# Attention over eight batches: the next batch's preparation placed among the units of the current one

## What is computed

```python
q = _split_heads(x @ Wq, h)
kv = _split_heads(x @ Wkv, h)
q = q * cos + _rotate_half(q) * sin
kv = kv * cos + _rotate_half(kv) * sin
q = q * d ** (-0.5)
kvs_ccs = jnp.concatenate([kvs[:, :-1], kvs[:, 1:]], axis=2)
lsim = jnp.einsum('csmd,csnd->csmn', qs[:, 1:], kvs_ccs)
lsim = jnp.concatenate([lsim[..., :m], jnp.where(causal, mask_value, lsim[..., m:])], axis=-1)
attn1 = jax.nn.softmax(lsim, axis=-1)
out1 = jnp.einsum('csij,csjd->csid', attn1, kvs_ccs)
out1 = _merge_heads(out1, b, h) @ Wo + bo
```

## Time and profile before

| | us |
|---|---|
| median of three runs | 3045.97 |
| the profiled execution, its own time | 3046.24 |
| its span | 3044.4 |
| TensorE busy | 2202.2 (72%) |
| VectorE busy | 2314.3 (76%) |
| ScalarE busy | 1553.2 (51%) |
| GpSimd busy | 845.2 (28%) |

### The profile page before, as it was taken

The page is one execution under the profiler, slowest core; times in us unless marked ns, Lnnn a source line. Parts: engine busy times, 40 slices in busy tenths (PEclk is TensorE's granted clock), DMA queues, the critical chain, the costliest instruction groups (busy, mean ns, idle before and its releaser), DMA issues. The chain is left out here.

```text
span 3044.4 us, 48644 instructions
## 1 busy us (share of the span) xinstructions
PE 2202.2 (72%) x12865; PEld 1704.6 (56%) x12865; DVE 2314.3 (76%) x5828; ACT 1553.2 (51%) x4161; POOL 845.2 (28%) x1482
## 2 busy tenths in 40 slices
PE   6787888786776878777777777877777775434676
PEld 3444454443444777666676766766766664333444
DVE  5555646556774199999999999999999999993566
ACT  3444434434664455555555555555555554443666
POOL 0000000000000144455544444544444554441000
PEclk8888978778888876677877777777767766565788
DMA  4000000000000000000000000000000000000000
GB/s 148 10 6 10 4 9 10 10 6 0 0 0 0 0 1 0 0 0 0 1 0 0 1 0 0 1 0 0 1 0 0 0 0 0 0 0 0 14 21 21
DMA packets 14137, 21.00 MB, mean 7 GB/s; under 512 B 1280, under 2 KB 12032, under 8 KB 13824
## 3 DMA queue, kind: packets, MB, share of 16 engines
q1 hardware_dynamic: 14080, 20.36, 2.2%
HBM read 12.27 MB, written 4.19 MB: 5 GB/s over the span
## 5 line engine op out<-in xcount | busy, mean ns | idle before, releaser
L1298 POOL TENSOR_TENSOR wu<-U,stg 128x256 f32<-128x256 f32 x512 | 317.8, 621 | 854.4 <-DVE U L1232 854.4
L556 PE MATMUL bank<-U,ident 128*128 128x128 f32 x2080 | 471.2, 398 | 115.4 <-ACT go L768 101.9
L556 PEld LDWEIGHTS bank<-U,ident 128*128 128x128 f32 x2080 | 434.2, 248 | 158.0 <-issue 72.9
L619 PE MATMUL bank<-stack,tm 128*128 128x64 f32 x1792 | 353.4, 387 | 217.4 <-ACT tm L705 217.4
L619 PEld LDWEIGHTS bank<-stack,tm 128*128 128x128 f32 x1792 | 341.9, 297 | 237.2 <-issue 237.2
L905 ACT ACTIVATE xs<-U 128x256 f32<-128x256 f32 x512 | 213.4, 417 | 468.9 <-DVE U L1232 467.4
L1182 DVE TENSOR_REDUCE pn<-xs 128x32 f32<-128x512 f32 x512 | 351.3, 686 | 29.3
L1251 POOL TENSOR_TENSOR stg<-R 128x128 f32 (+1 forms) x65 | 29.7, 457 | 1047.8 <-ACT stg L789 1047.8
L1255 POOL TENSOR_TENSOR kv<-stg 128x256 f32<-128x256 f32 x513 | 317.7, 619 | 1.7
L542 PE MATMUL bank<-wcat,yT 128*128 x1024 | 301.4, 454 | 3.0 <-issue 3.0
L677 ACT ACTIVATE prob<-bank,nmax 128x128 f32<-128x128 f32 x512 | 145.6, 366 | 247.6 <-DVE nmax L1026 246.6
(11 more groups left out here) (179 smaller groups left out, 3994.2 us busy)
## 6 DMA issues: line engine op xcount, KB each, us to landing
out_x<-x SPq DMA_DIRECT2D x8, 512.0 KB, 2.9
x<-in_x SPq DMA_DIRECT2D x1, 3584.0 KB, 16.8
Vs<-V SPq DMA_DIRECT2D x8, 272.0 KB, 3.4
lane<-in_lanes SPq DMA_DIRECT2D x8, 256.0 KB, 3.2
wcat<-in_wcat SPq DMA_DIRECT2D x1, 1792.0 KB, 14.0
Vs<-V SPq DMA_DIRECT2D x8, 204.0 KB, 2.7
wraw<-in_w_up SPq DMA_DIRECT2D x1, 1024.0 KB, 18.7
wraw<-in_w_down SPq DMA_DIRECT2D x1, 1024.0 KB, 10.9
```

Of the source, the lines that this page charges most:

```text
L556: last = pe.matmul(rsum.rearrange("p (t i) -> p t i", i=HD), ident[:, :], steps[:, :, :, j], start=(j == 0), stop=(j == HD - 1))
L619: last = pe.matmul(bank[3 + g][:, e * CH:(e + 1) * CH], tm[:, g * (PB // 2) + e, :, :].rearrange("p a c -> p (a c)"), stack[:, :], start=T ...
L1298: pool.tensor_tensor(ij(wu[:, :]), ij(U[:, half if j else 1 - half, (j - 1) % STEPS, :]), col(stg[:, half, j, TW, :]), ALU.mult).then_inc( ...
```

## The change

`KEEP` goes from 4 to 1, so the mask is written twice. `qT`, `kT`, `V` and `Vs` get a second copy, chosen by the batch's parity; the loop runs over pairs of batches. Batch 0 is prepared ahead of the loop. In the loop, the steps that prepare batch b+1 (`nxt`) stand between the steps of batch b's units, one tile in three slots. In the last iteration they prepare a batch that nothing reads. The normalisation of batch b+2 stands at the end of batch b. Banks change hands: projections use bank 3 alone, head transposes bank 0 alone, the values' product bank 2 alone, and o transposes and the output projection share bank 1. ScalarE copies both q and k. The square root of the variance goes to GpSimd as a power of one half. The scan moves from slot 3 to slot 17. On SyncE, the shift for batch b+1 stands behind the load of lane block b.

| slot w of batch b | TensorE | ScalarE | VectorE |
|---|---|---|---|
| 0 | row transposes of b+1 | | |
| 1 | | row copies | |
| 3, 6, 9, 12 | projection of tile 0 to 3 | | |
| 4, 7, 10, 13 | | | rotation |
| 5, 8, 11, 14 | | V and upper halves | |
| 6, 9, 12, 15 | | | lower halves |
| 7, 10, 13, 16 | transposes of q | | |
| 8, 11, 14, 17 | | copy of q | |
| 9, 12, 15, 18 | transposes of k | | |
| 10, 13, 16, 19 | | copy of k | |
| 13 | | absolute values | |
| 16, 17, 18 | | | statistics; scan; normalisation |

Within a slot VectorE now divides first (slots 5, 9, 13, 17), then takes the maximum, copies `probT`, and then does the steps of the table; the residual addition stays last (7, 11, 15, 19).

```diff
-KEEP = 4
+KEEP = 1
...
-        qT = sb("qT", [P, H // 2, L], F16, mid)
-        kT = sb("kT", [P, H // 2, SEG + L], F16, mid)
-        V = sb("V", [P, NT, H, HD + 1], F32, mid)
-        Vs = sb("Vs", [P, NT, H, HD + 1], F32, mid)
+        qT = sb("qT", [P, 2, H // 2, L], F16, mid)
+        kT = sb("kT", [P, 2, H // 2, SEG + L], F16, mid)
+        V = sb("V", [P, 2, NT, H, HD + 1], F32, mid)
+        Vs = sb("Vs", [P, 2, NT, H, HD + 1], F32, mid)
...  SyncE
+            def lanes_and_values(b, par_p, shift):
+                sp.wait_ge(w_car, b + 1)
+                sp.dma_start(lane[:, :], ...).then_inc(w_ld, 16)
+                if not shift:
+                    return
+                sp.wait_ge(A["v"], b * NT + 2 * NT)
+                shifted_values(par_p)
...  TensorE
+            def project_qkv(p, u):
+                if u == 0:
+                    pe.wait_ge(A["xc"], p * KD + KD)
+                else:
+                    pe.wait_ge(A["rp"], p * (6 * NT) + 6 * u)
+                for k in range(KD):
+                    last = pe.matmul(bank[3][:, :], xnT[:, k, u * P:(u + 1) * P], wqkv[:, k, :],
+                                     start=(k == 0), stop=(k == KD - 1))
+                last.then_inc(A["pj"], 1)
+            def transpose_heads(p, u, w):
+                pe.wait_ge(A["hiq"], p * (2 * NT) + 2 * u + w + 1)
+                pe.wait_ge(A["lo"], p * (2 * NT) + 2 * u + w + 1)
+                if w == 0:
+                    pe.wait_ge(A["kc"], p * NT + u)
+                    pe.wait_ge(A["xc"], p * KD + KD)
+                else:
+                    pe.wait_ge(A["qc"], p * NT + u + 1)
...
+                last.then_inc(A["qt"], 1)
+            rows_transposed(0)
+            project_qkv(0, 0)
+            for u in range(NT):
+                if u + 1 < NT:
+                    project_qkv(0, u + 1)
+                for w in range(2):
+                    transpose_heads(0, u, w)
+            with pe.Fori(0, B // 2) as pair:
+                for par_b in range(2):
...
+                        if w == 0:
+                            rows_transposed(nxt)
+                        if w >= 3 and w % 3 == 0 and w < 15:
+                            project_qkv(nxt, w // 3 - 1)
+                        if w >= 7 and (w - 7) % 3 == 0 and w < 19:
+                            transpose_heads(nxt, (w - 7) // 3, 0)
+                        if w >= 9 and (w - 9) % 3 == 0 and w < 21:
+                            transpose_heads(nxt, (w - 9) // 3, 1)
...  ScalarE
+            def split_heads(p, par_p, u):
+                act.wait_ge(A["zr"], p * NT + u + 1)
+                act.wait_ge(A["qt"], p * (2 * NT) + 2 * max(u - 1, 0))
...
+            copy_rows(0)
+            split_heads(0, 0, 0)
+            for u in range(NT):
+                if u + 1 < NT:
+                    split_heads(0, 0, u + 1)
+                for w in range(2):
+                    copy_heads(0, 0, u, w)
...
+                        if w == 1:
+                            copy_rows(nxt)
+                        if w >= 5 and (w - 5) % 3 == 0 and w < 17:
+                            split_heads(nxt, 1 - par_b, (w - 5) // 3)
+                        if w >= 8 and (w - 8) % 3 == 0 and w < 20:
+                            copy_heads(nxt, 1 - par_b, (w - 8) // 3, 0)
+                        if w >= 10 and (w - 10) % 3 == 0:
+                            copy_heads(nxt, 1 - par_b, (w - 10) // 3, 1)
...  VectorE
+                        if w >= 5 and (w - 5) % 4 == 0:
+                            u = (w - 5) // 4
+                            dve.wait_ge(A["pv"], b * 16 + 4 * u + 4)
...
+                        if w >= 4 and (w - 4) % 3 == 0 and w < 16:
+                            rotate(nxt, (w - 4) // 3)
+                        if w >= 6 and (w - 6) % 3 == 0 and w < 18:
+                            split_heads(nxt, (w - 6) // 3)
+                        if w == NT * 4:
+                            dve.wait_ge(A["x2"], b * NT)
+                            dve.wait_ge(A["xn"], b * NT + 2 * NT)
+                            layernorm_stats(pair * 2 + (par_b + 2), n2)
+                        if w == NT * 4 + 1:
+                            dve.wait_ge(w_abs, b + 1)
+                            dve.wait_ge(w_car, b + 1)
+                            dve.tensor_tensor_scan(lane[:, :], lane[:, :], lane[:, :], carry[:, 0:1], ALU.add,
+                                                   ALU.max).then_inc(w_scan, 1)
...
+                        if w == NT * 4 + 2:
+                            layernorm_apply(pair * 2 + (par_b + 2), n2)
...  GpSimd
+            with pool.Fori(2, B + 2) as q:
+                pool.wait_ge(A["ve"], q + 1)
+                pool.tensor_tensor(sd[:, 0, :], vv[:, 0, :], halves[:, :], ALU.pow).then_inc(A["sd"], 1)
```

More of the change, by code:

```diff
@@ L415, in _, with rows_transposed @@
             pe.wait_ge(ini, 6)
-            with pe.Fori(0, B) as b:
+            def rows_transposed(p):
+                pe.wait_ge(A["xn"], p * NT + NT)
+                pe.wait_ge(A["kc"], p * NT)
+                pe.wait_ge(A["rp"], p * (6 * NT))
                 for k in range(KD):
[L419 to L423, removed]
                     for u in range(NT):
-                        last = pe.transpose(bank[k][:, u * P:(u + 1) * P], xn[:, u, k * P:(k + 1) * P], ident[:, :])
+                        last = pe.transpose(bank[3 * k][:, u * P:(u + 1) * P], xn[:, u, k * P:(k + 1) * P], ident[:, :])
@@ L426, in _ @@
                     last.then_inc(A["xt"], 1)
[L427 to L441, removed]
-                            if v == 0:
[L443 to L453, removed]
@@ new lines, in project_qkv @@
+            def project_qkv(p, u):
[15 more added lines that the diff above has]
+                    pe.wait_ge(A["qc"], p * NT + u + 1)
+                dst = bank[0][:, :].bitcast(F16).rearrange("p (h t) -> p h t", t=P)
+                for hp in range(H // 2):
+                    last = pe.transpose(dst[:, hp, :],
+                                        qk4[:, u % 2, w, 2 * hp:2 * hp + 2, :, :].rearrange("p a c d -> p (a c d)"),
+                                        identh[:, :])
+                last.then_inc(A["qt"], 1)
@@ L637, in _, with copy_rows @@
         def _(act):
[L638 to L640 removed]
+            def copy_rows(p):
                 for k in range(KD):
[L642 to L685 removed]
@@ new lines, in _ @@
+            split_heads(0, 0, 0)
[4 more added lines that the diff above has]
+                    copy_heads(0, 0, u, w)
+            with act.Fori(0, B // 2) as pair:
+                for par_b in range(2):
+                    b = act.snap(pair * 2 + par_b)
+                    nxt = act.snap(pair * 2 + (par_b + 1))
+                    for w in range(NT * 4 + 4):
+                        if w < NT * 4:
+                            act.wait_ge(A["mx"], b * 16 + w + 1)
+                            if w >= 2:
+                                act.wait_ge(A["pt"], b * 16 + w - 1)
+                            else:
+                                act.wait_ge(A["pt"], b * 16)
+                            for i in range(4):
+                                last = act.activation(prob[:, w % 2, i, :], bank[6 + w % 2][:, i * P:(i + 1) * P], ACT.Exp,
+                                                      bias=nmax[:, w % 2, i:i + 1])
+                            last.then_inc(A["ex"], 1)
+                        if w >= 6 and (w - 6) % 4 == 0:
+                            u = (w - 6) // 4
+                            act.wait_ge(A["ot"], b * NT + u + 1)
+                            act.wait_ge(A["op"], b * NT + u)
+                            act.activation(oT_a[:, :, :], bank[1][:, 0:D].rearrange("p (k t) -> p k t", t=P),
+                                           ACT.Copy).then_inc(A["oc"], 1)
+                        if w == 1:
[6 more added lines that the diff above has]
+                            copy_heads(nxt, 1 - par_b, (w - 10) // 3, 1)
+                        if w == 13:
+                            act.wait_ge(w_ld, b * 16 + 16)
+                            act.activation(lane[:, :], lane[:, :], ACT.Abs).then_inc(w_abs, 1)
```

373 lines of the change are left out of this document (177 added, 196 removed).

## The result

Six runs of the changed kernel have a median of 3018.69 us (3015.8 to 3022.97), against 3045.97 before; the ratio is 0.9907, with a 95% interval of 0.9885 to 0.9929. The kernel became faster, as forecast, but by 0.9%, less than the 1% to which the prediction gave a chance of 0.91. The size was not right: 2916 was forecast, and the time lies outside the range of 2835 to 2990. The profiled execution took 3019.22 us, its span is 3017.4.

A forecast was written before the change was run, and what follows sets the result against it. Preparation and units in strict succession gave 87.6 us a batch; afterwards queue order, not any engine's sum, would set 66. 58 + 7 x 66 + 65.4 = 585.4 against 715.8 saves 130.4: 2916 us, range 2835 to 2990.

The forecast's parts named there:

- The walk through the slots, period 66: Attention loop's 20 slots, each engine strictly in program order: the next batch's first maximum starts at 66 us, before 87.6.
- The clock: TensorE's granted clock in the loop: 0.8 to 0.95 over a batch; doubled prices in first slots, about 2 of 66 us.
- Rival C: From each batch end's pause on, TensorE at half clock: period near 98, 3171 us, slower; decides from period 82; chance 0.06.
- The sign that I had set for an error: Loop period: below 60 would mean slack underrated, above 72 convoy; a loop clock under 0.75 also counted as wrong.
- Mask repeats, 10.2 us a batch less: Attention units, mask writes cut from five to two: units without three repeats take 59.4 - 10.2 = 49 us a batch.
- Table loads, 2.6 us a batch: Square root leaving ScalarE removes two table switches a batch, 1.28 us each, which stalled the units.
- Start: Batch 0's preparation before the loop, a serial chain of 9.1 us per tile at half clock: first maximum at 58, bounds 54 and 61.
- End of the batch: VectorE runs statistics 2.1, division 0.7, scan 4.65, normalisation 1.6, residual 0.9 unbroken; TensorE's drain and next scores lie under the scan.
- Value shift, memsets, last unused preparation: Shift costs zero, covered by the drain, else up to 4 us a batch; memsets about 2 us, hidden; last preparation no extra.
- E: Nothing hidden: one bank each makes every prepared tile stall the units; 30 us plus 49, period 79, 3019 us; chance 0.06.
- D: Convoy: waits in unit order serialise each preparation step instead of sharing; period 75, 59 us saved, 2987 us; chance 0.20.
- A: The forecast itself for the attention loop: period 62 to 70, total 2885 to 2945 us; chance 0.52.

## Why the prediction was wrong, step by step

**The walk through the slots, period 66: this step failed, by one wait.** The prediction names what holds the queues back: the rotations, the divisions, ScalarE's 1.15 + 1.5 + 1.0 in slots 8, 11 and 14. It does not name that the transposes of q write the bank from which ScalarE still copies the k of the tile before, behind the exponentials of the same slot, although `pe.wait_ge(A["kc"], p * NT + u)` stands in the diff. The two steps share slots 10, 13 and 16, and the wait shows in the first two, 1.8 and 3.7 us, 5.5 us a batch (44.2 / 8). 66 and 5.5 are 71.5. Moving the step restored 65.9, and with five writes, where the clock hardly changed, it was worth 5.6.

**The clock: named, and priced too low.** I doubled TensorE's prices only in the first slots of a batch, and the clock of the loop was forecast at 0.8 to 0.95 where 0.77 was measured. The missed wait made two pauses in the middle of each batch, and around them the clock fell to half, at the longer one always. The rest of the distance, 78.0 - 71.5 = 6.5 us a batch, goes with the clock over the batches shown above; it is a remainder and no direct measurement, and the pair with five writes, where it is absent, supports it. The loop's clock was 0.77 with the waits and two writes, 0.88 without the waits, and 0.91 with the waits and five writes. Rival C named the clock, but asked for a period of 82 in every batch; only one of seven got there. The sign that I had set for an error fired (a period above 72) and pointed to a convoy; the cause was this one wait and the clock behind it.

**Mask repeats, 10.2 us a batch less: wrong sign.** No run shows the 10.2 us, and no row of before the 2.05 us of a steady unit that stands in the 49.4. What the runs showed in their place: where TensorE is back to back at full clock in the changed kernel, the units start 2.04 us apart, and the two writes take 0.60 us to their last end where five took 1.25.

```profile
143.95 0.59 PE L498 MATMUL bank<-mask,identb 128*128 128x512 bf16 x2
...
145.99 0.60 PE L498 MATMUL bank<-mask,identb 128*128 128x512 bf16 x2
...
148.03 0.61 PE L498 MATMUL bank<-mask,identb 128*128 128x512 bf16 x2
```

So in such a unit the saving is there. In the units of the earlier trace rows TensorE is back to back too, but over the whole loop TensorE's busy time rose when three writes went, from 551.0 to 580.0 us, with the clock at 0.65. Where in the batch the repeats had held the clock up, the runs don't tell. Three of the five writes were worth 17 to 18 us net in either order as long as TensorE had the pauses; they cost 37 us once the wait on the k copy was gone.

**Table loads, 2.6 us a batch: not there.** Their removal alone brought no gain (3051.9 us).

**Start: nearly right.** 61.1 against 58, at the upper bound of 61, with 9.4 us a tile against the 9.1 of the chain (the rotations of tiles 2 and 3 start at 38.18 and 47.56, below).

```profile
38.18 0.42 DVE L1029 TENSOR_TENSOR zc<-bank,rope 128x256 f32<-128x256 f32 x1 [4.82 <-PE bank L448]
...
47.56 0.42 DVE L1029 TENSOR_TENSOR zc<-bank,rope 128x256 f32<-128x256 f32 x1 [4.81 <-PE bank L448]
```

**End of the batch: right on VectorE, incomplete on TensorE.** The unbroken run was there. The wait for issue at the return to the loop's head, 8.2 us in three returns, was not in the sum; in the old loop, with a shorter body, the transposes at its head had waited 8.9 us for issue in seven returns, 1.3 each. **Value shift, memsets, last unused preparation:** no cost of them is seen, as taken; no wait of TensorE on the shift is in the list. **Square root on GpSimd:** 1.0 us in place of 0.5, covered by the scan.

**The rivals.** E gave 3019 us for "one bank each makes every prepared tile stall the units", with 0.06. The time is that of E, and that is luck. E had 30 us of stalls on top of units of 49; measured are 5.5 us of waits on the shared bank, at two tiles of four, and a lower clock, and a change of one slot gave 83 us back. Of its mechanism only the shared bank was there. D's period of 75 was nearer than that of A, but no experiment showed its general convoy.

## What to carry to other kernels

When steps of a second chain are placed among those of a first, write for each shared buffer the slot of its last reader beside the slot of its next writer. Where the two slot numbers are equal, the writer can wait for all that stands ahead of the reader in that slot, and here the engine, which runs in order, kept everything behind it waiting, 1.8 and 3.7 us a batch. One slot of distance was enough here: 44.2 us of waits became 5.7. Look also at what the move puts beside the next batch: the last k copy became a new wait of 1.5 to 1.8 us. Price a repeat that keeps TensorE busy by an experiment in the order in which it will stand: here its worth went from 17 us gained to 37 us lost by a change of one slot elsewhere.

## What the runs showed that I had not expected

- A pause of 1.8 us of TensorE was followed by a fall to half clock in five batches and by none in three, for 6.8 to 13.7 us in the five; in or behind the pause of 3.7 us it fell in all eight. Equal batches of 596 instructions took 71.8 to 86.8 us, at clocks of 0.83 and 0.68.
- With five writes in the new order the periods alternate between 74.4 and 79.3 us, all seven of them: the second is the one with the return to the loop's head.
- GpSimd's power on 128 x 4 elements took 1.01 us.
